# Attention windows in another order, long exponentials kept in PSUM, low weight parts on GpSimd

## The chip, the cores and the metric

The kernel runs on one core of a Trainium2 chip. A core has TensorE (matmuls into PSUM, with its own weight loads), VectorE, ScalarE, GpSimd, and SyncE, which issues DMAs. The metric is the device time of one execution in microseconds (us).

## What is computed

A block of a transformer on x of shape (2, 1024, 512): a layer norm, then multi-head latent attention with 32 heads and a gated feed-forward, whose sum is added to x. The change touches the attention alone:

```python
q = (_rms_norm(x @ wq_a.T, q_norm_w) @ wq_b.T).reshape(b, s, NH, QK_NOPE + QK_ROPE)   # 32 heads, 128 + 64
q_pe = _apply_rope(q_pe, cos, sin); k_pe = _apply_rope(k_pe, cos, sin)
scores = (jnp.einsum('bshd,bthd->bhst', q_nope, k_nope) + jnp.einsum('bshd,btd->bhst', q_pe, k_pe)) * scale
scores = jnp.where(causal, scores, finfo.min)
out = jnp.einsum('bhst,bthd->bshd', softmax(scores), v).reshape(b, s, NH * V_DIM)
return out @ wo.T
```

## The kernel before

Three parts follow one another: `dense` (norm, feed-forward, latents), `attention`, and `combine` (the output product). Attention uses the latent form: keys and values stay as a shared latent of 64 columns, and each head's query weights are multiplied with its key weights first.

The work of attention is cut into 32 windows of 8 steps (`WINS`, `WIN`, `STEPS` = 256). A window is a pair of heads with one of the two batches; window w is pair w % 16 with batch w // 16, so all pairs of the first batch come before the second. Steps u = 0 to 3 are the first head, 4 to 7 the second. A step handles two query tiles of 128 rows: a long one with 8 to 5 key tiles (1024, 896, 768, 640 columns) and a short one with 1 to 4 (128 to 512 columns), 9 key tiles in all.

For each step s the engines do, in programs written out by hand with semaphores:

- TensorE: `scores(s, LONG)` into one half of `score_long` (two banks of PSUM of four, by s % 2), `scores(s, SHORT)`, `transposes(s - 1)` of the short exponentials into `flip`, `values(s - 5)` (27 matmuls into `acc`), and at some steps a projection piece (`project`, five matmuls for 512 query columns into `proj`), the latent weights (`absorb`) and `output_weights`. The long scores of step s wait for the long exponential of step s - 2, which has then read that half.
- VectorE: `least` gives the row minimum of either tile (scores are negated, so it is the shift), `outputs` divides, `low_long(s - 1)` and `low_short(s - 1)` form the low half of the exponentials split in two fp16 numbers, and once a window `weights_low` does so for the query weights.
- ScalarE: `exp` of both tiles, `high_short(s - 1)` and `high_long(s)` copy the high halves, `take` brings a projection piece from `proj` to SBUF, `query_high` makes the high half of rotated queries, and `weights_latent` and `weights_high` build the weights two windows ahead.
- GpSimd: for each half k of a window's queries (k = 2p for places 0 and 1 of window p, 2p + 1 for places 2 and 3) four DMAs that swap rotation halves (`swap_halves`, which waits for the two takes), then `query_low(k - 1)`, and the rotation (multiplications by `sinT` and `cosT`, additions).
- SyncE: the transposing DMA of the long exponentials (`turn`), weight loads and stores.

A window's four pieces are its places 0 to 3. `PIECE` says at which step which is projected: `0: (1, 3)` means that in step 0 the piece of place 3 of the window after this one is done. `HIGH` gives the steps of `query_high` for the next window. The first scores of a window wait until all four low query parts are there (`pe.wait_ge(ql_ready, 4 * w)`).

## Time and profile before

| | us |
|---|---|
| runs of the kernel (3) | 1512.58, 1525.0, 1527.79; median 1525.0 |
| profiled execution | 1517.88, its span 1516.1 |
| busy in the span | PE 1320.1, weight loads 905.5, DVE 1102.5, ACT 955.1, POOL 776.8 |

The profile is of one execution. PE is TensorE, PEld its weight loads, DVE VectorE, ACT ScalarE, POOL GpSimd, SP SyncE; L859 is line 859 of the kernel. A matmul's row overlaps the next one's, since they are pipelined: the distance between two starts is what one costs. Times on VectorE and ScalarE also overlap by about 0.1 us from row to row.

### The profile page before, as it was taken

Reading aid. Unit: us, or ns where it says so; the run is one execution under the profiler, and the core shown is the slowest. Engines: PE = TensorE matmul, PEld = TensorE weight load, DVE = VectorE, ACT = ScalarE, POOL = GpSimd, SP = SyncE. Lnnn points to the kernel's source line nnn. Section 1 sums busy time; section 2 is a strip of 40 time slices with the busy share of each in tenths; the row PEclk is TensorE's granted clock in tenths of the full one; section 3 lists DMA queues with packets and bytes.
Section 4 is the critical chain, followed back from the end, with each engine's and each line's share of the span. In section 5 each row is a group of like instructions: output and inputs, shape, how many; then the busy total and the mean of one; then the engine's idle time right before and its main releaser. Section 6 shows DMA issues by size and latency. Waiting matters only on the chain. (4 is left out here: it accounts for less than half of the span.)

```text
span 1516.1 us, 32860 instructions
## 1 busy us (share of the span) xinstructions
PE 1320.1 (87%) x13058; PEld 905.5 (60%) x13058; DVE 1102.5 (73%) x1664; ACT 955.1 (63%) x1690; POOL 776.8 (51%) x759
## 2 busy tenths in 40 slices
PE   4899995988989998999988899999889898479997
PEld 4787773666666666666666666666666666334443
DVE  3755454788888888888888888888888889542321
ACT  3644433777777777777777777777777778641120
POOL 0222011777677767767766776776776674000110
PEclk8999997999999999999999999999999999889999
DMA  4011004788899888799898888979888897799995
GB/s 158 29 56 57 28 21 138 136 161 145 155 173 171 163 147 157 157 162 173 153 161 152 155 159 163 167 159 172 141 161 154 157 168 139 178 182 228 247 244 131
DMA packets 573641, 225.85 MB, mean 149 GB/s; under 512 B 509232, under 2 KB 552880, under 8 KB 572848
## 3 DMA queue, kind: packets, MB, share of 16 engines
q1 hardware_dynamic: 562992, 199.09, 68.3%
q0 software_dynamic: 10496, 24.66, 7.2%
q8 instruction: 104, 1.70, 0.5%
q14 instruction: 49, 0.40, 0.1%
HBM read 55.91 MB, written 25.17 MB: 53 GB/s over the span
## 5 line engine op out<-in xcount | busy, mean ns | idle before, releaser
L737 ACT ACTIVATE prob_long_sb<-score_long,shift_sb 128x1024 f32<-128x1024 f32 (+3 forms) x256 | 245.0, 957 | 250.0 <-DVE shift_sb L853 249.8
L859 DVE TENSOR_TENSOR prob_hl_sb<-prob_long_sb,prob_hl_sb 128x1024 f16<-128x1024 f32 (+3 forms) x256 | 358.0, 1398 | 0.0
L853 DVE TENSOR_REDUCE shift_sb<-score_long 128x1 f32<-128x1024 f32 (+3 forms) x256 | 259.4, 1013 | 68.1 <-PE score_long L649 67.6
L828 POOL TENSOR_TENSOR ql_sb<-qf_sb,qh_sb 128x512 f16<-128x512 f32 x124 | 144.8, 1169 | 233.9 <-ACT qh_sb L757 233.9
L745 ACT ACTIVATE prob_hl_sb<-prob_long_sb 128x1024 f16<-128x1024 f32 (+3 forms) x256 | 232.5, 908 | 0.0
L646 PE MATMUL score_long<-key_hi,qh_sb 128*128 128x512 f16 (+3 forms) x512 | 176.3, 344 | 10.0 <-DVE ql_sb L914 9.1
L659 PE MATMUL flip<-ident_sb,prob_short_sb 128*128 128x128 f32 x640 | 117.4, 281 | 73.9 <-DVE ptl_short_sb L865 73.7
L845 POOL TENSOR_TENSOR qf_sb<-qf_sb,rot_sb 64x512 f32<-64x512 f32 x124 | 174.1, 1404 | 9.5
L821 POOL DMA_DIRECT2D rot_sb<-qf_sb x248 | 124.8, 508 | 104.6 <-DVE ql_sb L914 61.3
L680 PE MATMUL acc<-ch,prob_t_sb 128*128 128x65 f16 x1664 | 177.5, 192 | 0.0
L678 PE MATMUL acc<-ch,prob_t_sb 128*128 128x65 f16 x1664 | 177.2, 194 | 0.3 <-DMA prob_t_sb<-prob_hl_sb 0.3
L679 PE MATMUL acc<-cl,prob_t_sb 128*128 128x64 f16 x1664 | 177.3, 191 | 0.0
L841 POOL TENSOR_TENSOR qf_sb<-qf_sb,cosT_sb 128x512 f32<-128x512 f32 x124 | 176.4, 1442 | 0.0
L647 PE MATMUL score_long<-key_lo,qh_sb 128*128 128x512 f16 (+3 forms) x512 | 174.6, 341 | 0.0
L648 PE MATMUL score_long<-key_hi,ql_sb 128*128 128x512 f16 (+3 forms) x512 | 171.1, 341 | 0.0
L680 PEld LDWEIGHTS acc<-ch,prob_t_sb 128*128 128x128 f16 x1664 | 153.1, 97 | 0.0
L679 PEld LDWEIGHTS acc<-cl,prob_t_sb 128*128 128x128 f16 x1664 | 152.7, 98 | 0.0
L678 PEld LDWEIGHTS acc<-ch,prob_t_sb 128*128 128x128 f16 x1664 | 152.2, 97 | 0.4 <-DMA prob_t_sb<-prob_hl_sb 0.4
L659 PEld LDWEIGHTS flip<-ident_sb,prob_short_sb 128*128 128x128 f32 x640 | 68.5, 140 | 115.9 <-issue 110.1
L865 DVE TENSOR_TENSOR ptl_short_sb<-flip,pth_short_sb 128x128 f16<-128x128 f32 (+3 forms) x256 | 123.9, 484 | 18.6 <-ACT pth_short_sb L752 9.7
L737 ACT ACTIVATE prob_short_sb<-score_short,shift_sb 128x128 f32<-128x128 f32 (+3 forms) x256 | 133.9, 523 | 0.0
L632 PE MATMUL proj<-lat_hi,wq_h_sb 128*128 128x512 f32 x246 | 107.2, 436 | 23.6 <-issue 22.9
(180 smaller groups left out, 3396.8 us busy)
## 6 DMA issues: line engine op xcount, KB each, us to landing
o<-o_sb SPq DMA_DIRECT2D x32, 512.0 KB, 4.5
o_nat_sb<-o SPq DMA_DIRECT2D x32, 512.0 KB, 6.8
rot_sb<-qf_sb POOLq DMA_DIRECT2D x248, 64.0 KB, 3.5
wqk_sb<-wqk SPq DMA_DIRECT2D x32, 320.0 KB, 4.4
wo_sb<-wo SPq DMA_DIRECT2D x16, 512.0 KB, 4.2
x_sb<-x SPq DMA_DIRECT2D x4, 1024.0 KB, 4.8
y<-y_sb SPq DMA_DIRECT2D x16, 256.0 KB, 2.0
wq_f_sb<-wqp SPq DMA_DIRECT2D x32, 128.0 KB, 4.5
```

What stands on the lines that cost most here:

```text
L646: nc.tensor.matmul(out, qh[:, row, q], key_hi[:, head, at], start=True, stop=False)
L647: nc.tensor.matmul(out, qh[:, row, q], key_lo[:, head, at], start=False, stop=False)
L659: mm = nc.tensor.transpose(flip[:, at], prob[SHORT][:, s % 2, at], ident[:])
L678: nc.tensor.matmul(acc[:, at:at + KVL + 1], hi, high, start=(j == 0), stop=False)
L679: nc.tensor.matmul(acc[:, at:at + KVL], hi, low, start=False, stop=False)
L680: mm = nc.tensor.matmul(acc[:, at:at + KVL + 1], lo, high, start=False, stop=(j == i))
L737: nc.scalar.activation(prob[kind][:, s % 2, 0:width(s, kind)], score_of(s, kind), ACT.Exp, bias=shift[:, s % (2 * WIN), kind:kind + 1], sc ...
L745: nc.scalar.activation(prob_hl[:, s % NHL, 0:n], prob[LONG][:, s % 2, 0:n], ACT.Copy).then_inc(hi_ready, 1)
L841: op = nc.gpsimd.tensor_tensor(qf[:, c, h, :], qf[:, c, h, :], cosT[:, h, at], ALU.mult)
L845: nc.gpsimd.tensor_tensor(qf[rows, c, h, :], qf[rows, c, h, :], rot[rows, c, :], ALU.add).then_inc(rot_add, 1)
L853: nc.vector.tensor_reduce(shift[:, s % (2 * WIN), kind:kind + 1], score_of(s, kind), AX.X, ALU.min).then_inc(shift_ready[kind], 1)
L859: nc.vector.tensor_tensor(prob_hl[:, s % NHL, n:2 * n], prob[LONG][:, s % 2, 0:n], prob_hl[:, s % NHL, 0:n], ALU.subtract).then_inc(lo_rea ...
```

## The change

- Window w is now pair w // 2 with batch w % 2. Both batches of a pair use the same query weights, so they are built (`absorb`, `weights_latent`, `weights_high`) in every second window (`new_pair`) and loaded half as often.
- The long exponential is written over its scores in PSUM. `prob_long` is gone, `high_long` and `low_long` read PSUM, and the long scores of a step wait for `lo_ready`, the long low part of the step two before.
- `weights_low` moves from VectorE to GpSimd, all but the first.
- `PIECE` puts places 0 and 1 at steps 4 and 6 instead of 3 and 4. Of these two pieces TensorE does three of five matmuls at the end of the step before (`BEGUN`).
- VectorE's order in a step becomes long minimum, long low part, short minimum, short low part, outputs. ScalarE's begins with `high_short(s - 1)`.

```diff
--- before.py
+++ after.py
@@ -483,7 +483,7 @@
...
-        prob = [sb("prob_short", [P, 2, 512], F32), sb("prob_long", [P, 2, S], F32)]
+        prob = sb("prob_short", [P, 2, 512], F32)
         prob_hl = sb("prob_hl", [P, NHL, 2 * S], F16)
...
@@ -521,8 +521,9 @@
...
-        PIECE = {0: (1, 3), 3: (2, 0), 4: (2, 1), 7: (2, 2)}
-        PIECE_FIRST = {0: (1, 2), 1: (1, 3), 4: (2, 0), 5: (2, 1), 7: (2, 2)}
+        PIECE = {0: (1, 3), 4: (2, 0), 6: (2, 1), 7: (2, 2)}
+        PIECE_FIRST = {0: (1, 2), 1: (1, 3), 4: (2, 0), 6: (2, 1), 7: (2, 2)}
+        BEGUN, TERMS = {4: 3, 6: 3}, 5
         HIGH = {1: (0,), 2: (1,), 5: (2,), 6: (3,)}
@@ -536,6 +537,11 @@
...
             return [4 * pair + n for n in (HIGH_FIRST if pair == 1 else HIGH).get(s % WIN, ())] if pair < WINS else []
+        def new_pair(w):
+            p = 1 if w == 0 else (w + 3) // 2 if w % 2 == 1 else PAIRS
+            return p if p < PAIRS else None
@@ -543,8 +549,8 @@
...
                 j = p % 2
-                sp.dma_start(raw[j][:].rearrange("p h c -> p (h c)"), io["wqk"][:, p % PAIRS, :]).then_inc(w_in[j], 16)
-                sp.dma_start(wf[j][:, :, KVL:KVL + 2 * ROPE], io["wqp"][:, p % PAIRS, :, :]).then_inc(w_in[j], 16)
+                sp.dma_start(raw[j][:].rearrange("p h c -> p (h c)"), io["wqk"][:, p, :]).then_inc(w_in[j], 16)
+                sp.dma_start(wf[j][:, :, KVL:KVL + 2 * ROPE], io["wqp"][:, p, :, :]).then_inc(w_in[j], 16)
@@ -570,7 +576,7 @@
...
                 sp.wait_ge(o_ready, BLK * (w + 1))
-                sp.dma_start(scr["o"][w % PAIRS, w // PAIRS], o[:, w % 2].rearrange("p t c -> p (t c)")).then_inc(o_out[w % 2], 16)
+                sp.dma_start(scr["o"][w // 2, w % 2], o[:, w % 2].rearrange("p t c -> p (t c)")).then_inc(o_out[w % 2], 16)
@@ -581,18 +587,18 @@
...
                 swap_halves(k)
-            for j in range(2):
-                sp.wait_ge(wl_ready, j + 1)
-                load_w(2 + j)
+            sp.wait_ge(wl_ready, 1)
+            load_w(2)
             for s in range(STEPS):
...
                     load_wo((w + 1) // 2)
-                if u == 3 and w + 4 < WINS:
-                    sp.wait_ge(wl_ready, w + 3)
-                    load_w(w + 4)
+                p = new_pair(w)
+                if u == 4 and p is not None and p + 2 < PAIRS:
+                    sp.wait_ge(wl_later, p)
+                    load_w(p + 2)
                 if u == LAG and w >= 1:
@@ -620,22 +626,23 @@
...
-            def project(n, out=proj[:]):
+            def project(n, out=proj[:], first=0, end=TERMS):
...
                 p, c, h = n // 4, n // 2 % 2, n % 2
-                b, j = p // PAIRS, p % 2
+                b, j = p % 2, p // 2 % 2
                 cols = slice(h * P, (h + 1) * P)
...
                 terms = ((wh, 0, lat_hi, 0), (wh, 0, lat_lo, 0), (wl, 0, lat_hi, 0), (wh, 1, lat_hi, 1), (wl, 1, lat_hi, 1))
-                for i, (w, t, q, kind) in enumerate(terms):
-                    mm = nc.tensor.matmul(out, w[j][:, t, cols], q[:, kind, at], start=(i == 0), stop=(i == 4))
-                mm.then_inc(proj_mm, 1)
+                for i, (w, t, q, kind) in list(enumerate(terms))[first:end]:
+                    mm = nc.tensor.matmul(out, w[j][:, t, cols], q[:, kind, at], start=(i == 0), stop=(i == TERMS - 1))
+                if end == TERMS:
+                    mm.then_inc(proj_mm, 1)
...
                 pair, head, i = s // WIN, s % WIN // BLK, tile(s, kind)
-                b = pair // PAIRS
+                b = pair % 2
                 q, row = slice(i * P, (i + 1) * P), 2 * (pair % 2) + head
@@ -656,11 +663,11 @@
...
                     at = slice(j * P, (j + 1) * P)
-                    mm = nc.tensor.transpose(flip[:, at], prob[SHORT][:, s % 2, at], ident[:])
+                    mm = nc.tensor.transpose(flip[:, at], prob[:, s % 2, at], ident[:])
                 mm.then_inc(flip_mm, 1)
...
             def values(s):
-                b = s // WIN // PAIRS
+                b = s // WIN % 2
                 for kind in (SHORT, LONG):
@@ -681,12 +688,9 @@
...
             absorb(0)
-            pe.wait_ge(lat_ready, 1)
-            absorb(1)
             pe.wait_ge(wl_ready, 1)
...
                 project(n, score_long[:, n, :])
-            pe.wait_ge(wl_ready, 2)
             project(4)
@@ -698,7 +702,7 @@
...
                     if s >= 2:
-                        pe.wait_ge(exp_ready[LONG], s - 1)
+                        pe.wait_ge(lo_ready, s - 1)
                     scores(s, LONG)
@@ -714,27 +718,34 @@
...
                     n = piece_at(s)
-                    if n is not None:
+                    if n is not None and u in BEGUN:
+                        project(n, first=BEGUN[u])
+                    elif n is not None:
+                        pe.wait_ge(proj_out, n)
+                        project(n)
+                    if u + 1 in BEGUN and piece_at(s + 1) is not None:
+                        n = piece_at(s + 1)
                         pe.wait_ge(proj_out, n)
                         if n % 4 == 0:
-                            pe.wait_ge(wl_ready, n // 4 + 1)
+                            pe.wait_ge(wl_later, n // 8)
                             pe.wait_ge(wo_ready, w + 1)
-                        project(n)
+                        project(n, end=BEGUN[u + 1])
                     if absorb_at(s):
...
                             pe.wait_ge(wo_ready, w)
-                        if w + 2 < WINS:
-                            absorb(w + 2)
+                        if new_pair(w) is not None:
+                            absorb(new_pair(w))
                         output_weights(w)
...
                 act.wait_ge(shift_ready[kind], s + 1)
-                if s >= 2:
-                    act.wait_ge(lo_ready if kind == LONG else flip_mm, s - 1)
-                nc.scalar.activation(prob[kind][:, s % 2, 0:width(s, kind)], score_of(s, kind), ACT.Exp,
+                if kind == SHORT and s >= 2:
+                    act.wait_ge(flip_mm, s - 1)
+                out = score_of(s, LONG) if kind == LONG else prob[:, s % 2, 0:width(s, SHORT)]
+                nc.scalar.activation(out, score_of(s, kind), ACT.Exp,
                                      bias=shift[:, s % (2 * WIN), kind:kind + 1], scale=-1.0).then_inc(exp_ready[kind], 1)
@@ -742,7 +753,7 @@
...
                 n = width(s, LONG)
-                nc.scalar.activation(prob_hl[:, s % NHL, 0:n], prob[LONG][:, s % 2, 0:n], ACT.Copy).then_inc(hi_ready, 1)
+                nc.scalar.activation(prob_hl[:, s % NHL, 0:n], score_of(s, LONG), ACT.Copy).then_inc(hi_ready, 1)
@@ -770,9 +781,8 @@
...
-            for p in range(2):
-                weights_latent(p)
-                weights_high(p)
+            weights_latent(0)
+            weights_high(0)
             for n in range(4):
@@ -783,10 +793,10 @@
...
                 w, u = s // WIN, s % WIN
+                if s >= 1:
+                    high_short(s - 1)
                 exp(s, LONG)
                 exp(s, SHORT)
-                if s >= 1:
-                    high_short(s - 1)
                 high_long(s)
@@ -799,12 +809,12 @@
...
                     act.wait_ge(vo_mm, w + 1)
-                    if w + 2 < WINS:
-                        weights_latent(w + 2)
+                    if new_pair(w) is not None:
+                        weights_latent(new_pair(w))
                     nc.scalar.activation(wo_out[:, w // 2, w % 2 * H // 2:(w % 2 + 1) * H // 2], of_out, ACT.Copy,
                                          scale=kvw2[:, 0:1]).then_inc(wo_ready, 1)
-                if high_weights_at(s) and w + 2 < WINS:
-                    weights_high(w + 2)
+                if high_weights_at(s) and new_pair(w) is not None:
+                    weights_high(new_pair(w))
             high_short(STEPS - 1)
@@ -828,6 +838,11 @@
...
+            def weights_low(p):
+                pool.wait_ge(wh_ready, p + 1)
+                nc.gpsimd.tensor_tensor(wl[p % 2][:], wf[p % 2][:], wh[p % 2][:].bitcast(F32),
+                                        ALU.subtract).then_inc(wl_later, 1)
             for k in range(2, 2 * WINS):
@@ -835,6 +850,8 @@
...
                     query_low(k - 1)
+                if c == 1 and new_pair(k // 2 - 1) is not None:
+                    weights_low(new_pair(k // 2 - 1))
                 pool.wait_ge(rot_in[c], 64 * (k // 2))
@@ -856,7 +873,7 @@
...
                 n = width(s, LONG)
-                nc.vector.tensor_tensor(prob_hl[:, s % NHL, n:2 * n], prob[LONG][:, s % 2, 0:n], prob_hl[:, s % NHL, 0:n],
+                nc.vector.tensor_tensor(prob_hl[:, s % NHL, n:2 * n], score_of(s, LONG), prob_hl[:, s % NHL, 0:n],
                                         ALU.subtract).then_inc(lo_ready, 1)
@@ -888,8 +905,7 @@
...
                 nc.vector.tensor_copy(to[:], of[:]).then_inc(cast_ready, 1)
-            for p in range(2):
-                weights_low(p)
+            weights_low(0)
@@ -918,15 +934,15 @@
...
                     least(s, LONG)
+                if 1 <= s <= STEPS:
+                    low_long(s - 1)
+                if s < STEPS:
                     least(s, SHORT)
+                if 1 <= s <= STEPS:
+                    low_short(s - 1)
                 t = s - LAG
...
                     outputs(t)
-                if 1 <= s <= STEPS:
-                    low_long(s - 1)
-                    low_short(s - 1)
-                if s < STEPS and high_weights_at(s) and w + 2 < WINS:
-                    weights_low(w + 2)
```

Where the rows move, engine by engine. First VectorE, the third step of a window (long tile of the step before 896 columns); L853 and L870 are `least`, L859 and L876 `low_long`. Before:

```order
L853 TENSOR_REDUCE shift_sb<-score_long 128x1 [waits score_long]
L853 TENSOR_REDUCE shift_sb<-score_short 128x1 [waits score_short]
L879 RECIPROCAL rtot_sb<-acc 128x4 [waits pv_mm]
L884 TENSOR_TENSOR o_sb<-acc,rtot_sb 128x2x2x64 [waits rtot_ready]
L859 TENSOR_TENSOR prob_hl_sb<-prob_long_sb,prob_hl_sb 128x896 [waits hi_ready]
L865 TENSOR_TENSOR ptl_short_sb<-flip,pth_short_sb 128x256 [waits pth_ready]
L870 TENSOR_TENSOR wq_l_sb<-wq_f_sb,wq_h_sb 128x512 [waits wh_ready]
```

Now:

```order
L870 TENSOR_REDUCE shift_sb<-score_long 128x1 [waits score_long]
L876 TENSOR_TENSOR prob_hl_sb<-score_long,prob_hl_sb 128x896 [waits hi_ready]
L870 TENSOR_REDUCE shift_sb<-score_short 128x1 [waits score_short]
L882 TENSOR_TENSOR ptl_short_sb<-flip,pth_short_sb 128x256 [waits pth_ready]
L896 RECIPROCAL rtot_sb<-acc 128x4 [waits pv_mm]
L901 TENSOR_TENSOR o_sb<-acc,rtot_sb 128x2x2x64 [waits rtot_ready,o_out1]
```

The long low part now stands behind the long minimum, ahead of the short one and of the outputs, takes its input from `score_long`, and the weights' row (before: L870) is gone.

Second ScalarE, from the take of place 0 or 1 in step 4 of a window to step 6 (L762 and L773 are `take`, L757 and L768 `query_high`, L752 and L763 `high_short`). Before, the first row is the take of place 1:

```order
L762 ACTIVATE qf_sb<-proj 128x512 [waits proj_mm,ql_ready]
L737 ACTIVATE prob_long_sb<-score_long,shift_sb 128x896 [waits lo_ready,shift_long]
L737 ACTIVATE prob_short_sb<-score_short,shift_sb 128x256 [waits flip_mm,shift_short]
L752 ACTIVATE pth_short_sb<-flip 128x128 [waits flip_mm,pv_mm]
L745 ACTIVATE prob_hl_sb<-prob_long_sb 128x896 [waits exp_long,turn_in1]
L757 ACTIVATE qh_sb<-qf_sb 128x512 [waits rot_add]
L737 ACTIVATE prob_long_sb<-score_long,shift_sb 128x768 [waits lo_ready,shift_long]
L737 ACTIVATE prob_short_sb<-score_short,shift_sb 128x384 [waits flip_mm,shift_short]
L752 ACTIVATE pth_short_sb<-flip 128x256 [waits flip_mm,pv_mm]
L745 ACTIVATE prob_hl_sb<-prob_long_sb 128x768 [waits exp_long,turn_in2]
L757 ACTIVATE qh_sb<-qf_sb 128x512 [waits rot_add]
```

Now, the first row is the take of place 0, and that of place 1 stands in step 6:

```order
L773 ACTIVATE qf_sb<-proj 128x512 [waits proj_mm,ql_ready]
L763 ACTIVATE pth_short_sb<-flip 128x128 [waits flip_mm,pv_mm]
L748 ACTIVATE score_long<-score_long,shift_sb 128x896 [waits shift_long]
L748 ACTIVATE prob_short_sb<-score_short,shift_sb 128x256 [waits flip_mm,shift_short]
L756 ACTIVATE prob_hl_sb<-score_long 128x896 [waits exp_long,turn_in1]
L768 ACTIVATE qh_sb<-qf_sb 128x512 [waits rot_add]
L763 ACTIVATE pth_short_sb<-flip 128x256 [waits flip_mm,pv_mm]
L748 ACTIVATE score_long<-score_long,shift_sb 128x768 [waits shift_long]
L748 ACTIVATE prob_short_sb<-score_short,shift_sb 128x384 [waits flip_mm,shift_short]
L756 ACTIVATE prob_hl_sb<-score_long 128x768 [waits exp_long,turn_in2]
L773 ACTIVATE qf_sb<-proj 128x512 [waits proj_mm,ql_ready]
L768 ACTIVATE qh_sb<-qf_sb 128x512 [waits rot_add]
```

The take of place 1 has moved behind the long high copy of step 6, ahead of the last `query_high`; the short high copy leads each step. GpSimd's own order around these is unchanged: the four DMAs that wait for this take, then the two `query_low` of the window to come, and now in every second window `weights_low` behind the pair of `query_low` in its middle.

Third TensorE, where the pieces of a new window begin, at the end of step 3. Before:

```order
L632 MATMUL proj<-lat_hi,wq_h_sb 128x512 [waits wo_ready,wl_ready,proj_out]
L632 MATMUL proj<-lat_lo,wq_h_sb 128x512
L632 MATMUL proj<-lat_hi,wq_l_sb 128x512
L632 MATMUL proj<-lat_hi,wq_h_sb 128x512
L632 MATMUL proj<-lat_hi,wq_l_sb 128x512
L646 MATMUL score_long<-key_hi,qh_sb 128x512 [waits exp_long]
```

Now:

```order
L638 MATMUL proj<-lat_hi,wq_h_sb 128x512 [waits wo_ready,wl_later,proj_out]
L638 MATMUL proj<-lat_lo,wq_h_sb 128x512
L638 MATMUL proj<-lat_hi,wq_l_sb 128x512
L653 MATMUL score_long<-key_hi,qh_sb 128x512 [waits lo_ready]
L654 MATMUL score_long<-key_lo,qh_sb 128x512
```

Three of the five matmuls stand ahead of the scores of step 4, with the wait for the low weights (`wl_later`, set by GpSimd), and the scores wait for `lo_ready` in place of `exp_long`. The first scores of a window wait for `ql_ready` too, as before.

## Rows read from the trace of the kernel before

**Rows 1.** Busy time of each engine in one stretch of attention, 100 us long.

```profile
core 0: us, PE busy (x) PEld busy (x) DVE busy (x) ACT busy (x) POOL busy (x), PEclk, DMA share, GB/s
500.00:600.00 100.00, 90.28 (x1077) 62.81 (x1075) 87.14 (x126) 76.10 (x133) 70.29 (x66) 1.00 0.88 163
```

**Rows 2.** Timeline of TensorE, one window: start us, us, instruction, [idle before it].

```profile
586.80 0.39 PE L646 MATMUL score_long<-key_hi,qh_sb 128*128 128x512 f16 x1
...
588.10 0.22 PE L649 MATMUL score_long<-mask_b_sb,ident_b_sb 128*128 128x128 bf16 x1
...
589.64 0.47 PE L632 MATMUL proj<-lat_hi,wq_h_sb 128*128 128x512 f32 x1
...
590.90 0.39 PE L646 MATMUL score_long<-key_hi,qh_sb 128*128 128x512 f16 x1
...
593.88 1.08 PE L611 MATMUL proj<-wqk_sb 128*128 128x64 f32 x8
594.89 0.65 PE L619 MATMUL proj<-wo_sb,wv_sb 128*64 128x256 f32 x4
595.47 0.39 PE L646 MATMUL score_long<-key_hi,qh_sb 128*128 128x512 f16 x1
...
598.10 0.38 PE L646 MATMUL score_long<-key_hi,qh_sb 128*128 128x512 f16 x1
...
619.71 0.39 PE L646 MATMUL score_long<-key_hi,qh_sb 128*128 128x512 f16 x1
```

**Rows 3.** Waits of TensorE, 200 to 1400 us: total us, times, longest.

```profile
PE flip L659 <- DVE ptl_short_sb L865: 73.7, 157, 1.8
```

**Rows 4.** Costliest groups, whole run, then by form, 400 to 1300 us.

```profile
L859 DVE TENSOR_TENSOR prob_hl_sb<-prob_long_sb,prob_hl_sb 128x1024 f16<-128x1024 f32 (+3 forms) x256 | 358.0, 1398 | 0.0
...
L859 DVE TENSOR_TENSOR prob_hl_sb<-prob_long_sb,prob_hl_sb 128x640 f16<-128x640 f32 x55 | 97.9, 1780 | 0.0
...
L865 DVE TENSOR_TENSOR ptl_short_sb<-flip,pth_short_sb 128x512 f16<-128x512 f32 x55 | 37.3, 678 | 0.3 <-ACT pth_short_sb L752 0.2
```

**Rows 5.** Timeline of VectorE in the last window, GpSimd idle.

```profile
1290.06 1.22 DVE L853 TENSOR_REDUCE shift_sb<-score_long 128x1 f32<-128x1024 f32 x1
...
1292.34 0.82 DVE L859 TENSOR_TENSOR prob_hl_sb<-prob_long_sb,prob_hl_sb 128x640 f16<-128x640 f32 x1
...
1295.14 1.21 DVE L859 TENSOR_TENSOR prob_hl_sb<-prob_long_sb,prob_hl_sb 128x1024 f16<-128x1024 f32 x1
...
1298.83 1.08 DVE L859 TENSOR_TENSOR prob_hl_sb<-prob_long_sb,prob_hl_sb 128x896 f16<-128x896 f32 x1
...
1301.49 0.94 DVE L859 TENSOR_TENSOR prob_hl_sb<-prob_long_sb,prob_hl_sb 128x768 f16<-128x768 f32 x1
```

**Rows 6.** Timeline of ScalarE and GpSimd, steps 4 to 6 of the window.

```profile
609.90 0.60 ACT L762 ACTIVATE qf_sb<-proj 128x512 f32<-128x512 f32 x1
...
610.80 2.01 POOL L821 DMA_DIRECT2D rot_sb<-qf_sb  x4 [1.39 <-ACT qf_sb L762]
...
616.75 0.66 ACT L757 ACTIVATE qh_sb<-qf_sb 128x512 f16<-128x512 f32 x1
...
617.48 1.16 POOL L828 TENSOR_TENSOR ql_sb<-qf_sb,qh_sb 128x512 f16<-128x512 f32 x1 [1.62 <-ACT qh_sb L757]
```

**Rows 7.** Timeline of VectorE and ScalarE in step 6.

```profile
614.37 0.55 DVE L853 TENSOR_REDUCE shift_sb<-score_short 128x1 f32<-128x384 f32 x1
...
615.28 0.60 ACT L737 ACTIVATE prob_short_sb<-score_short,shift_sb 128x384 f32<-128x384 f32 x1
...
616.01 0.87 ACT L745 ACTIVATE prob_hl_sb<-prob_long_sb 128x768 f16<-128x768 f32 x1
```

**Rows 8.** Timeline of TensorE and ScalarE in the first window.

```profile
271.18 0.38 PE L646 MATMUL score_long<-key_hi,qh_sb 128*128 128x512 f16 x1
...
274.50 0.63 ACT L771 ACTIVATE wq_h_sb<-wq_f_sb 128x512 fp32r<-128x512 f32 x1
...
290.88 0.39 PE L646 MATMUL score_long<-key_hi,qh_sb 128*128 128x512 f16 x1 [0.74 <-POOL ql_sb L828]
```

2 lines of the change are left out of this document (1 added, 1 removed).

## Prediction

> **What bounds the kernel now.** I read the table of stretches first, then TensorE's own rows step by step, then the waits. Attention is 256 steps; eight steps are one window (a head pair with one batch), and it is nearly the whole span between about 256 and 1310 us. In a stretch of it TensorE is busy 90%, VectorE 87%, ScalarE 76%, GpSimd 71%, with TensorE's clock granted in full [rows 1]. No engine is full, so I looked for what repeats. The window from 586.80 to 619.71 takes 32.91 us [rows 2], and the windows around it take the same within 0.1 us. I number its steps 0 to 7. Step 0 takes 4.10 us with one projection piece, step 2 takes 2.63 us, and both run without a wait. A piece costs 1.26 us (589.64 to 590.90), the latent weights 1.01 us, the output weights 0.58 us [rows 2]. Every step has the same number of score and value columns and differs only in 1 to 4 transposes: from 4.10 - 1.26 = 2.84 us with four and 2.63 us with two, a step without extras is 2.84, 2.52, 2.63, 2.74 us. Two of each, four pieces (5.04), 1.01 and 0.58 give 28.1 us. So 4.8 us of each window are waits. The largest named one is for VectorE's short low parts [rows 3]. VectorE is late because its subtraction of the long low parts is slow while GpSimd works: 1398 ns in the mean, 1780 ns for 640 columns [rows 4], against 0.82 us for the same shape after GpSimd's last rotation [rows 5].
>
> **VectorE.** The subtraction now reads the long exponentials in PSUM. Its nearest row is the same operation for the short tile, PSUM in, 678 ns for 512 columns [rows 4], no slower a column than the undisturbed long rows once the fixed part is taken off. Below them I see no reason for a gain; above, the 1.40 us of now would be the other end, were it PSUM and not GpSimd's company that counts. I take the undisturbed durations of [rows 5]: 1.21, 1.08, 0.94 and 0.82 us for 1024 down to 640 columns, where the mean over the attention is 1.40 [rows 4]. That frees 0.39 us a step, 3.1 us a window, and the low weights leave VectorE too, which is then no bound.
>
> **TensorE.** Sharing weights between the two batches drops the latent weights in every second window: 28.1 becomes 27.6 us on average. The pieces are the same work in other places: step 3 gets three of five matmuls (0.76 us), step 4 two (0.50), 5 and 6 likewise, steps 7 and 0 a whole one.
>
> **The new hold on the scores.** Scores of step s+1 now wait for the long low part of step s-1, and not for an exponential. VectorE does this part right behind the minimum of step s, which waits for the scores of step s. So one step can't be shorter than long scores, minimum, subtraction. Long scores take 1.52 us at 1024 columns (586.80 to the mask row's end at 588.32) and 0.16 less a tile [rows 2]; the minimum takes 1.22 us for 1024 [rows 5] and like the subtraction for the others. With 0.11 us for handoffs and overlap (an estimate), steps 0 to 3 need 3.67, 3.76, 3.34 and 2.90 us, and 4 to 7 the same. Taking the larger of this and TensorE's own work: 4.11, 3.76, 3.34, 3.50, 3.67, 3.76, 3.34, 4.00, in all 29.5 us, and 0.35 more in every second window, where step 1 holds the latent weights. ScalarE's work is 25 us of it (76% of 32.9, [rows 1]) and loses half of its weight copies, so it isn't the bound. If nothing else stood in the way, 29 windows would save 3.2 us each, some 93 us.
>
> **What stands in the way.** One move undoes this. GpSimd issues the four swap DMAs of a pair only when its places 0 and 1 are taken, and does the low query parts of the next window behind them. Before, place 1 was taken in step 4: ScalarE ended at 610.50, the DMAs began at 610.80 and took 2.01 us, and the two low parts (1.16 us each) then waited only for ScalarE's high parts and ended at 618.64, 1.07 us before the next window's scores at 619.71 [rows 6]. Now place 1 is taken in step 6. Behind this take lie 0.30 us to GpSimd, 2.01 us for the DMAs and 2 x 1.16 us, and scores of the next window wait for all four low parts. Step 6 begins 22.1 us into the window by the sum above (22.5 in every second). In it come scores (1.24 with the handoff), minimum 0.95, subtraction 1.08, short minimum 0.55, short exponential 0.60, high copy 0.85, take 0.60, less 0.37 for rows that begin before the former's end: 5.5 us [rows 2, 5, 7]. To this the 4.63 us of GpSimd and about 0.15 to TensorE. The next window begins at 22.1 + 5.5 + 4.8 = 32.4 us, or 32.8 us. TensorE would stand for some 3 us at each window's start, and of 3.2 us only about 0.35 us remain: 29 windows of 32.91 us, 954.4 us, become 14 x 32.4 + 15 x 32.76 = 945, so some 10 us are won.
>
> **The ends.** In the first window the three terms of step 3 wait for the low weights, now on GpSimd behind its two low query parts and not on VectorE. The high weights of [rows 8] end at 275.1 and come half a microsecond later in the new order; GpSimd ends at about 278.1. And this wait now stands ahead of the scores of step 4, which were at 271.18. I get 279.0 for them, 286.4 for step 6 and, with the same tail of 10.3 us, 296.7 for the second window, where it was 290.88 [rows 8]: 5.8 us lost. The window before the last has no later take and wins 0.5 us; the last, where nothing disturbed VectorE before, loses about 1.5 us to the hold. Sum: -10 + 5.8 - 0.5 + 1.5 = -3 us. Against the profiled execution (1517.9 us, its span 1516.1) that is 1515 us; that execution lies inside the runs (median 1525.0), from which it would be 1522. I predict **1518 us**. Anything within 1% of 1525 is no change that a measurement of this kernel can tell.
>
> **Bounds of what no row shows.** No instruction in the trace writes PSUM from ScalarE. Nearest are its copies and exponentials that read PSUM: the exponential on 384 columns takes 0.60 us [rows 7]. A write in place could cost nothing more, or, if reading and writing the same banks take turns, the time again. Below nothing I exclude more than some 0.05 us each, the scale of fixed parts in these rows. I take nothing. The Trainium skill, "ScalarEngine: Activation LUTs", section on what happens when an exp runs, says PSUM is the lower-latency destination for ScalarE; no row shows it, and it would leave the sum where it is, since the long exponential of step 6 is ready 0.6 us before it is needed. GpSimd's low weights are bounded by its own two-input rows, 1.16 us [rows 6], and hidden in the middle of a window. Each of the dozen handoffs on the ring may be off by 0.03 us: 0.4 us a window, 12 us in all.
>
> **Rivals.** (1) *The ring through GpSimd has slack that I don't see*, say because the low parts aren't needed or the take is earlier. Then the windows run at 29.7 us: 1518 - 93 = 1425 us. For it speaks that VectorE's relief is certain; against it, the order of GpSimd's instructions, and that this very wait shows once already: the scores at 290.88, ahead of which both low parts came late, stood 0.74 us for them [rows 8]. Chance 0.08. (2) *Slower: the exponential in place costs double.* Its four shapes average some 0.95 us, so ScalarE gets 7.6 us more per window, 25 becomes near 32, and the take of step 6, the end of ScalarE's chain, comes 1 to 2 us late. It decides from the point where the long exponential costs over 0.6 us more. 29 x 1.5 = 44: 1562 us. Chance 0.08. (3) *The hold is longer than I make it*: the subtraction has to wait for ScalarE's high copy in steps 2, 3 and 6, where I find only 0.2 to 0.5 us to spare. For it speaks that the copy of short tiles now stands ahead of both exponentials; against it, that ScalarE is idle a quarter of the time [rows 1]. +0.9 us a window, 1544 us. Chance 0.10. (4) *TensorE has room*: if its rows overstate it, the steps 0 and 3, where I let its own work decide, shrink to the hold (3.67, 2.90), 1.0 us a window before the ring: 1489 us. Against it stand step 0 and step 2, whose rows lie end to end. Chance 0.06. The Trainium skill, "Perfetto Trace Analysis", on identifying the most-contended engine, would have TensorE judged by weight loads, and [rows 1] have them at 63% beside 90% for matmuls: by that rule (4) it is. (5) *Ring right, quicker round*: my walk is too long by 0.4 us a window or more: 1495 to 1508 us, chance 0.13. My forecast, 1508 to 1540, has the remaining 0.55.
>
> **How the numbers follow.** Faster by over 1% (below 1510): cases 1, 4, 5 and a sliver of mine, 0.28. Slower by over 1% (above 1540): case 2 and most of 3, 0.16. Within: 0.56. The range reaches over (3) and (4) and leaves (1) and (2) out: 1484 to 1548.
>
> **What would show it.** In the profile after: each window near 32.5 us; TensorE idle some 3 us before the long scores of every eighth step, released by GpSimd's low query part; the swap DMAs right behind the take of step 6, and the low parts right behind them; the long subtraction at 0.82 to 1.21 us; VectorE near 75% busy; GpSimd's multiplications shorter, since nothing disturbs them; the first window near 40 us. The prediction is wrong if windows are near 29.5 us without that idle time, or if the long exponentials take well over 1.1 us at 1024 columns.

## The result and the profile after

The changed kernel takes 1563.2 us, median of 4 runs (1558.66 to 1569.87), against 1524.9 us of the kernel before (4 runs, 1512.58 to 1527.79): a ratio of 1.027, 95% interval 1.0212 to 1.0328. It is slower, and outside the range that was given. Its profiled execution took 1561.21 us, span 1559.4. Here and below a median is that of all runs of a kernel, and a ratio leaves out the few that were in a slower state of the chip.

The table of stretches of the changed kernel: the one that answers to [rows 1], and 3.2 us of two windows:

```profile
core 0: us, PE busy (x) PEld busy (x) DVE busy (x) ACT busy (x) POOL busy (x), PEclk, DMA share, GB/s
500.00:600.00 100.00, 89.79 (x1039) 63.11 (x1038) 70.14 (x117) 73.19 (x126) 64.36 (x68) 0.96 0.85 157
...
598.40:601.60 3.20, 3.20 (x38) 3.12 (x36) 2.98 (x6) 1.68 (x3) 2.52 (x3) 0.51 0.47 91
632.10:635.30 3.20, 3.20 (x44) 2.46 (x42) 3.12 (x6) 2.42 (x4) 0.42 (x1) 1.00 0.90 75
```

VectorE fell from 87% to 70% busy, and TensorE stays at 90%. The same share hides that it did less: 1039 matmuls where there were 1077. And the granted clock is no longer full. Both short stretches begin 1.5 us after a window's first scores and show TensorE fully busy, but the granted clock is 0.51 in the first (1.2 GHz) and 1.00 in the second (2.4 GHz). Full busy time says nothing of the speed.

TensorE's timeline at the same two places (the answer to [rows 2]), where each first row opens a window and each second one opens its step 1:

```profile
596.88 0.39 PE L653 MATMUL score_long<-key_hi,qh_sb 128*128 128x512 f16 x1 [2.48 <-POOL ql_sb L838]
...
602.57 0.39 PE L653 MATMUL score_long<-key_hi,qh_sb 128*128 128x512 f16 x1
...
630.59 0.39 PE L653 MATMUL score_long<-key_hi,qh_sb 128*128 128x512 f16 x1 [2.48 <-POOL ql_sb L838]
...
634.67 0.39 PE L653 MATMUL score_long<-key_hi,qh_sb 128*128 128x512 f16 x1
```

Both windows open after the same 2.48 us without work, released by GpSimd's low query part, as the prediction has it. But step 0, with the same work, takes 5.69 us behind the first and 4.08 behind the second. In 26 of the 29 windows from the second to the thirtieth it is the longer one. The record of the clock shows a dip, of some 3.4 us (6.8 in one), in each of these 26. The kernel before shows none between 290 and 1314 us; its waits of about the same sum (4.8 us a window) lie in pieces of 1.9 us or less.

The round through GpSimd itself (called the ring below: take, four swap DMAs, two low query parts, next scores), in the window from 630.59 to 663.12 (timeline of ScalarE, GpSimd and TensorE, beside [rows 6]):

```profile
657.89 0.60 ACT L773 ACTIVATE qf_sb<-proj 128x512 f32<-128x512 f32 x1
...
658.77 2.00 POOL L831 DMA_DIRECT2D rot_sb<-qf_sb  x4 [3.46 <-ACT qf_sb L773]
...
660.79 2.27 POOL L838 TENSOR_TENSOR ql_sb<-qf_sb,qh_sb 128x512 f16<-128x512 f32 x2
...
663.12 0.61 PE L653 MATMUL score_long<-key_hi,qh_sb 128*128 128x512 f16 x1 [2.49 <-POOL ql_sb L838]
```

The take of place 1 ends at 658.49, and 4.63 us later the next window's scores begin. GpSimd's two low parts follow the four DMAs without a gap, so the wait is this queue and nothing else. In one window, from 764.83, GpSimd starts its four DMAs late without a cause that the profile names (797.66, 3.3 us behind the take's end at 794.37); it takes 3.0 us more than its like. The trace of before has the same 3.3 us once, at 778.45.

The long subtraction and the exponential (groups of the whole run, then by form, 400 to 1200 us, beside [rows 4] and [rows 5]):

```profile
L876 DVE TENSOR_TENSOR prob_hl_sb<-score_long,prob_hl_sb 128x1024 f16<-128x1024 f32 (+3 forms) x256 | 259.6, 1014 | 2.0 <-ACT prob_hl_sb L756 2.0
L748 ACT ACTIVATE score_long<-score_long,shift_sb 128x1024 f32<-128x1024 f32 (+3 forms) x256 | 238.8, 933 | 18.0 <-DVE shift_sb L870 17.7
...
L748 ACT ACTIVATE score_long<-score_long,shift_sb 128x1024 f32<-128x1024 f32 x47 | 51.1, 1087 | 0.0
...
L876 DVE TENSOR_TENSOR prob_hl_sb<-score_long,prob_hl_sb 128x640 f16<-128x640 f32 x47 | 38.3, 814 | 0.0
```

The subtraction takes 1014 ns in the mean where it was 1398, and 814 for 640 columns where it was 1780. The exponential in place costs nothing more (933 ns in the mean, 957 before).

The first window on TensorE, beside [rows 8]:

```profile
250.69 0.59 PE L653 MATMUL score_long<-key_hi,qh_sb 128*128 128x512 f16 x1 [9.14 <-DVE ql_sb L930]
...
272.45 0.77 PE L638 MATMUL proj<-lat_hi,wq_h_sb 128*128 128x512 f32 x1 [6.64 <-POOL wq_l_sb L843]
273.87 0.65 PE L653 MATMUL score_long<-key_hi,qh_sb 128*128 128x512 f16 x1
...
292.59 0.39 PE L653 MATMUL score_long<-key_hi,qh_sb 128*128 128x512 f16 x1 [2.49 <-POOL ql_sb L838]
```

**The account**, by starts of windows in the two profiled executions, changed against before. The first scores come at 250.69, not 256.33: -5.6 us. The first window takes 41.90, not 34.55: +7.4. The 29 windows after it take 983.05, not 955.94: +27.1. With step 0 at 4.1 us in all of them they would take some 941 (983.1 less 26 x 1.6, an estimate), fewer than before. The last two come to -0.3. The output part behind attention takes 216.6 us, not 201.8: +14.8. In all 43.3, the difference of the spans.

### The profile page after: what moved, and what is told of

Same layout as the page of the kernel before. It is cut to its first block and busy times, and to the rows that moved or that the text cites. A ratio compares the mean times of both kernels' runs of the same rounds, so it can differ in the third digit from the quotient of the medians.

```text
span 1559.4 us, 32254 instructions
## 1 busy us (share of the span) xinstructions
PE 1334.1 (86%) x12930; PEld 907.7 (58%) x12930; DVE 956.4 (61%) x1633; ACT 950.7 (61%) x1658; POOL 721.4 (46%) x774
## 5 line engine op out<-in xcount | busy, mean ns | idle before, releaser
L870 DVE TENSOR_REDUCE shift_sb<-score_long 128x1 f32<-128x1024 f32 (+3 forms) x256 | 261.7, 1022 | 311.6 <-PE score_long L656 307.9
L876 DVE TENSOR_TENSOR prob_hl_sb<-score_long,prob_hl_sb 128x1024 f16<-128x1024 f32 (+3 forms) x256 | 259.6, 1014 | 2.0 <-ACT prob_hl_sb L756 2.0
L748 ACT ACTIVATE score_long<-score_long,shift_sb 128x1024 f32<-128x1024 f32 (+3 forms) x256 | 238.8, 933 | 18.0 <-DVE shift_sb L870 17.7
L763 ACT ACTIVATE pth_short_sb<-flip 128x128 f16<-128x128 f32 (+3 forms) x256 | 112.5, 440 | 190.0 <-PE flip L666 187.2
L756 ACT ACTIVATE prob_hl_sb<-score_long 128x1024 f16<-128x1024 f32 (+3 forms) x256 | 221.5, 865 | 0.3
L653 PEld LDWEIGHTS score_long<-key_hi,qh_sb 128*128 128x128 f16 x512 | 50.3, 98 | 238.4 <-POOL ql_sb L838 91.2
L654 PE MATMUL score_long<-key_lo,qh_sb 128*128 128x512 f16 (+3 forms) x512 | 182.1, 356 | 0.0
L655 PE MATMUL score_long<-key_hi,ql_sb 128*128 128x512 f16 (+3 forms) x512 | 180.2, 358 | 0.0
L862 POOL TENSOR_TENSOR qf_sb<-qf_sb,rot_sb 64x512 f32<-64x512 f32 x124 | 157.0, 1266 | 9.5
L858 POOL TENSOR_TENSOR qf_sb<-qf_sb,cosT_sb 128x512 f32<-128x512 f32 x124 | 155.7, 1278 | 0.0
L1030 PE MATMUL sum<-woh_sb,oT_sb 128*128 128x512 f16 x256 | 100.2, 391 | 26.9 <-DMA oT_sb<-o_hl_sb 26.1
```

Source lines behind the costliest of these rows:

```text
L653: nc.tensor.matmul(out, qh[:, row, q], key_hi[:, head, at], start=True, stop=False)
L654: nc.tensor.matmul(out, qh[:, row, q], key_lo[:, head, at], start=False, stop=False)
L655: nc.tensor.matmul(out, ql[:, row, q], key_hi[:, head, at], start=False, stop=not last)
L748: nc.scalar.activation(out, score_of(s, kind), ACT.Exp, bias=shift[:, s % (2 * WIN), kind:kind + 1], scale=-1.0).then_inc(exp_ready[kind], 1)
L756: nc.scalar.activation(prob_hl[:, s % NHL, 0:n], score_of(s, LONG), ACT.Copy).then_inc(hi_ready, 1)
L858: op = nc.gpsimd.tensor_tensor(qf[:, c, h, :], qf[:, c, h, :], cosT[:, h, at], ALU.mult)
```

## The experiments

The kernel before ran beside each group of four: 1523.6, 1523.4 and 1521.8 us. Where a run is called "with pieces back" it is this one:

**Pieces back at their old steps.** Everything of the change stays but the fourth point of its list, the one on `PIECE` (the first window's pieces and the waits go with it).

```diff
-        PIECE = {0: (1, 3), 4: (2, 0), 6: (2, 1), 7: (2, 2)}
...
-        BEGUN, TERMS = {4: 3, 6: 3}, 5
+        PIECE = {0: (1, 3), 3: (2, 0), 4: (2, 1), 7: (2, 2)}
...
+        BEGUN, TERMS = {}, 5
...
                         pe.wait_ge(proj_out, n)
+                        if n % 4 == 0:
+                            pe.wait_ge(wl_later, n // 8)
+                            pe.wait_ge(wo_ready, w + 1)
                         project(n)
```

> The changed kernel with the projection pieces back at steps 0, 3, 4 and 7, whole, and nothing else undone. Theory (ring and clock: the take of place 1 in step 6 delays the swap DMAs and the low query parts behind it, TensorE stands 2.84 us at each window's start and then runs some 3.4 us at half clock, 1.6 us more): no wait for the low query parts, clock 1.00 throughout attention, steps of 4.1, 3.7 or 4.1, 3.3, 4.0, 4.1, 3.7, 3.3, 4.0 us, windows of 30.3 us where the changed kernel has 33.7 and 34.15. 29 windows x 3.65 = 106 us and 6 us of the first window: about 1450 us. Rival (the hold on the score banks is what costs): windows stay near 33 us or above, 1530 us or more.

Measured: 1459.6 us (0.957 of before, 0.952 to 0.961). Its windows take 30.47 and 30.90 us in turn, TensorE doesn't wait for a low query part at a window's start (0.3 us once, at the second), and its clock is 1.00 from 400 to 1200 us. So two pieces placed later cost 103.6 us, which is more than the whole loss. Between the spans it is 109.2, and the 29 windows hold 93.5 of it.

**The same move by itself in the kernel before.**

```diff
-        PIECE = {0: (1, 3), 3: (2, 0), 4: (2, 1), 7: (2, 2)}
...
+        PIECE = {0: (1, 3), 4: (2, 0), 6: (2, 1), 7: (2, 2)}
...
+        BEGUN, TERMS = {4: 3, 6: 3}, 5
...
```

> The kernel before with this one part of the change alone: places 0 and 1 in steps 4 and 6, three of five matmuls a step early. Ring theory: the same wait for the low query parts at each window's start, the same half clock behind it, windows of 35 to 36 us where they were 32.9: 1590 to 1615 us. Rival (the ring needs the other parts of the change): within 1% of 1525 us.

Measured: 1617.6 us (1.061, 1.055 to 1.066). From its trace, a window's first step:

```profile
653.91 0.39 PE L648 MATMUL score_long<-key_hi,qh_sb 128*128 128x512 f16 x1 [2.12 <-POOL ql_sb L836]
...
659.59 0.39 PE L648 MATMUL score_long<-key_hi,qh_sb 128*128 128x512 f16 x1
```

Much the same wait (2.12 us for 2.48) and 5.68 us behind it. Step 0 is the slow one in 17 of 29 windows; the other 12 took 4.10 there. The move costs 94 us here and 104 above: most of its cost doesn't depend on the rest of the change.

**The clock alone: work in the idle time.** In step 7 the piece is computed three times; only the third counts. The ring stays.

```diff
-            def project(n, out=proj[:], first=0, end=TERMS):
+            def project(n, out=proj[:], first=0, end=TERMS, signal=True):
...
-                if end == TERMS:
+                if end == TERMS and signal:
                     mm.then_inc(proj_mm, 1)
...
                         pe.wait_ge(proj_out, n)
+                        for _ in range(2 if u == 7 else 0):
+                            project(n, signal=False)
                         project(n)
```

> The changed kernel with its wait left in, and TensorE does the piece of step 7 three times over (ten more matmuls of 0.23 us, the same values into the same bank, only the last signalled), so that it isn't idle for more than about 0.4 us of the 2.84. If the clock is what makes step 0 cost 5.7 in place of 4.1 us: the granted clock stays at 1.00, step 0 is back at 4.1 us, windows near 32.3 us, 1563 - 26 x 1.6 = 1521 us, though TensorE has 2.5 us more work in each window. Rival (step 0 is slow for another reason, such as the DMAs of that time, or the wait grows by the extra work): no gain or a loss, 1563 us or more.

Measured: 1525.7 us (1.0008 of before, 0.998 to 1.0037), 37.6 us less than the changed kernel though TensorE does more. Its stretch and the first two steps of a window:

```profile
500.00:600.00 100.00, 96.26 (x1123) 67.60 (x1122) 73.60 (x124) 77.25 (x131) 68.63 (x71) 1.00 0.86 162
```

```profile
616.01 0.39 PE L653 MATMUL score_long<-key_hi,qh_sb 128*128 128x512 f16 x1 [0.19 <-POOL ql_sb L840]
...
620.10 0.39 PE L653 MATMUL score_long<-key_hi,qh_sb 128*128 128x512 f16 x1
```

Step 7 still lasts 6.88 us (6.84 in the changed kernel), so the ring sets the same time. But step 0 is back at 4.09, and the 29 windows take 943.8 us where the changed kernel's take 983.1. The 39.3 us between are the clock's price, 1.5 us for each of the 26 slow steps. The prediction had 945 us for these windows. It described this kernel, not the changed one. That it is met within 1.2 us is in part luck: the regular windows take 32.15 and 32.58 us, 0.2 less than predicted, and one stretch with GpSimd's late start (35.56 and 33.78 us, with a half-clock step) gives 5 us back.

**Low parts ahead of the DMAs.** On GpSimd, the last two low query parts of the next window go first, and the swap DMAs of the window after it follow.

```diff
+                if k > 2 and c == 0:
+                    query_low(k - 1)
                 swap_halves(k)
-                if k > 2:
+                if k > 2 and c == 1:
                     query_low(k - 1)
```

> The changed kernel with its pieces where they are, but GpSimd does the two low query parts of a window ahead of the four swap DMAs of the next (for the halves with places 0 and 1). Ring and clock theory: the low parts then wait only for the last high part of step 6, TensorE's wait at a window's start falls from 2.8 us to 0.1 or nothing, the clock stays, windows of 29.6 us: 1563 - 29 x 4.35 = 1437 us. Rival (TensorE waits there because the take, or GpSimd as a whole, is late): some 1 to 2 us of the wait stay and windows are near 32 us, 1510 us.

Measured: 1535.4 us (1.0065, 1.003 to 1.010), a miss of nearly 100 us. The wait at the window's start went (step 7 4.20 us, step 0 4.10), but step 3 now takes 4.5 to 11.2 in 27 of 29 windows, and the granted clock falls at 13 of these waits too. GpSimd and then ScalarE in its trace:

```profile
583.57 1.17 POOL L838 TENSOR_TENSOR ql_sb<-qf_sb,qh_sb 128x512 f16<-128x512 f32 x1 [2.71 <-ACT qh_sb L768]
584.67 2.01 POOL L831 DMA_DIRECT2D rot_sb<-qf_sb  x4
594.84 1.27 POOL L858 TENSOR_TENSOR rot_sb<-rot_sb,sinT_sb 128x512 f32<-128x512 f32 x1 [8.16 <-DMA rot_sb<-qf_sb]
...
598.63 2.59 POOL L864 TENSOR_TENSOR qf_sb<-qf_sb,rot_sb 64x512 f32<-64x512 f32 x2
```

```profile
599.92 0.63 ACT L768 ACTIVATE qh_sb<-qf_sb 128x512 f16<-128x512 f32 x1 [5.59 <-POOL qf_sb L864]
```

The DMAs leave at a window's end, land up to 8 us later, the rotation follows, and ScalarE stands at `query_high` in step 1 with all exponentials behind it. I had looked at one side of the queue only.

**The same, with `query_high` of places 0 and 1 a step later.**

```diff
-        HIGH = {1: (0,), 2: (1,), 5: (2,), 6: (3,)}
+        HIGH = {2: (0,), 3: (1,), 5: (2,), 6: (3,)}
```

> The changed kernel with the two low query parts ahead of the swap DMAs (which alone gave 1535.4 us and an irregular wait of 4.5 to 11 us in step 3), and ScalarE's query_high of places 0 and 1 one step later (steps 2 and 3, not 1 and 2). If that wait is ScalarE standing at query_high because the swap DMAs leave only in step 7 and land up to 8 us later, it shrinks by one step, 3.3 us: windows mostly at 29.9 to 31 us and the kernel at 1445 to 1470 us. Rival: the irregular wait has another source (the DMA queues, TensorE's clock); then it stays and the time is again near 1535 us.

Measured: 1455.3 us (0.954, 0.948 to 0.960). Step 3 is regular again (3.7 us), and every second window takes 29.91 us. The others take 29.46 at best and up to 32.9: their step 7 takes 4.2 to 7.6, where ScalarE stands at the `query_high` of step 5 behind DMAs that land late. So the wait in step 3 was ScalarE's place in that queue. 29.46 and 29.91 are the window that the prediction gave without anything in the way (29.5, and 29.85 every second).

**Pieces split, from the walk.** Pieces back, but three of five matmuls of those in steps 3 and 7 are done a step earlier, where the hold left TensorE idle.

```diff
-        BEGUN, TERMS = {}, 5
+        BEGUN, TERMS = {3: 3, 7: 3}, 5
```

> The changed kernel with the pieces back at their old steps 0, 3, 4 and 7, but three of the five matmuls of the pieces of steps 3 and 7 done at the end of steps 2 and 6. In the run with whole pieces at these steps, steps 2 and 6 took 3.25 us, which is the hold on the score banks (TensorE's own work there is 2.63), and steps 3 and 7 took 4.20, which is TensorE's own work. If the walk of the prediction holds (each step the larger of hold and own work), steps 2 and 6 become 3.4 and steps 3 and 7 some 3.5, so a window 30.7 - 1.1 = 29.6 us and the kernel 1459.6 - 29 x 1.1 = 1428 us. Rival: the round through GpSimd binds at once when windows shrink; then the windows stay above 30.3 and the kernel at 1448 or more, with TensorE waiting for the low query part again and its clock falling behind that.

Measured: 1423.6 us (0.934, 0.927 to 0.940), windows 29.10 and 29.53.

**And place 1 over steps 4 and 5.**

```diff
-        PIECE = {0: (1, 3), 3: (2, 0), 4: (2, 1), 7: (2, 2)}
-        BEGUN, TERMS = {3: 3, 7: 3}, 5
+        PIECE = {0: (1, 3), 3: (2, 0), 5: (2, 1), 7: (2, 2)}
+        BEGUN, TERMS = {3: 3, 5: 3, 7: 3}, 5
```

> As the run before (pieces split over 2 and 3, 6 and 7), and place 1 spread over steps 4 and 5, taken in step 5 and no longer in step 4. The take moves one step, not two as in the changed kernel. The ring of the prediction from a take in step 5 (it starts at about 18.1 us of the window): take's end about 5.9 us later, 0.30, 2.01, 2 x 1.16, 0.15: 28.8 us, below the window of 29.1 that the hold and TensorE's own work give. So no wait at the window's start, 0.4 us a window less than the run before: 1428 - 12 = 1416 us. Rival: the swap DMAs, which now leave 4 us later, land too late for the rotation behind them (in the trace with low parts first they took up to 8 us), query_high then holds ScalarE, and the kernel comes out above 1440 us.

Measured: 1414.6 us (0.927, 0.921 to 0.932), the fastest of all. A window of 29.06 us on TensorE, without idle time ahead of either row:

```profile
577.90 0.39 PE L653 MATMUL score_long<-key_hi,qh_sb 128*128 128x512 f16 x1
...
606.96 0.39 PE L653 MATMUL score_long<-key_hi,qh_sb 128*128 128x512 f16 x1
```

One step later fits into the ring, two steps don't. Its matmuls are 98% busy from 500 to 600 us. The idea of spreading the pieces was sound; the place of one take was not.

**What the other parts bring.** Four more runs, which lead from the kernel before to the one with pieces back. First the orders of VectorE and ScalarE alone:

```diff
                     least(s, LONG)
+                if 1 <= s <= STEPS:
+                    low_long(s - 1)
+                if s < STEPS:
                     least(s, SHORT)
...
+                if s >= 1:
+                    high_short(s - 1)
                 exp(s, LONG)
                 exp(s, SHORT)
-                if s >= 1:
-                    high_short(s - 1)
```

> The kernel before with only the new orders: VectorE long minimum, long low part, short minimum, short low part, outputs; ScalarE with the short high copy first. Windows, weights, pieces and the long exponentials in SBUF stay as they were. The run with pieces back and long exponentials in SBUF (1463.8 us) has these orders, shared weights and low weights on GpSimd over before, 60 us in all. Theory 1, the orders bring most of it, since the short low parts for which TensorE's transposes waited 73.7 us come earlier: 1475 to 1490 us. Theory 2, VectorE's load is what counts (87% busy, low weights in every window), and an order adds nothing to it: 1510 to 1530 us.

Measured: 1524.6 us (1.0017, 0.9996 to 1.0038). No gain, theory 2. Added to it, the exponential in place:

```diff
-                        pe.wait_ge(exp_ready[LONG], s - 1)
+                        pe.wait_ge(lo_ready, s - 1)
...
+                out = score_of(s, LONG) if kind == LONG else prob[SHORT][:, s % 2, 0:width(s, SHORT)]
...
```

> The run before this one (the new orders alone) with the long exponential written over its scores in PSUM, and the long scores waiting for the low part. VectorE then has the subtraction at 1010 ns and not 1400, 3 us a window, while its low weights are still there in every window. Theory of the prediction: VectorE's time was the bound, the hold sets 29.5 to 31 us a window, with whole pieces in steps 3 and 4 near 31: 1524 - 29 x 1.9 = about 1470 us. Rival: in the kernel with shared weights and pieces back the same step changed nothing (1463.8 to 1459.6); if that is general, this run equals the one with the orders alone.

Measured: 1504.9 us (0.989, 0.986 to 0.992): 20 us, not the 54 expected and not nothing. Its steps are those of the longer windows of the run with pieces back but for step 3, 5.68 us for 4.20. There TensorE stands ahead of the next pair's first piece until VectorE has made the low weights, which it does in every window here:

```profile
561.73 1.23 DVE L871 TENSOR_TENSOR wq_l_sb<-wq_f_sb,wq_h_sb 128x512 fp32r<-128x512 f32 x1 [1.50 <-ACT wq_h_sb L772]
...
563.07 0.47 PE L632 MATMUL proj<-lat_hi,wq_h_sb 128*128 128x512 f32 x1 [1.02 <-issue]
```

Then, with pieces back, the long exponentials in SBUF:

```diff
-                        pe.wait_ge(lo_ready, s - 1)
+                        pe.wait_ge(exp_ready[LONG], s - 1)
...
-                out = score_of(s, LONG) if kind == LONG else prob[:, s % 2, 0:width(s, SHORT)]
+                out = prob_long[:, s % 2, 0:width(s, LONG)] if kind == LONG else prob[:, s % 2, 0:width(s, SHORT)]
...
```

> The run with the pieces back at their old steps (1459.6 us), with the long exponentials in SBUF again: the subtraction reads two SBUF inputs, and the long scores wait for an exponential and not for the low part. If the exponentials in PSUM pay by VectorE's relief, the subtraction is back at some 1400 ns in the mean (1780 for 640 columns) and the windows go from 30.7 to about 31.9 us (the old 32.9, less 0.9 of low weights that stay on GpSimd, 0.1 of shared weights): 1459.6 + 35 = 1495 us. Rival: the hold on the score banks costs as much as the relief gives; then steps 5 and 6 fall from 3.69 and 3.25 to near TensorE's own 2.7 and the kernel is at 1455 us or below.

Measured: 1463.8 us (0.960, 0.953 to 0.966), against 1459.6, and the two kernels' runs overlap: neither theory. By form, 400 to 1200 us, this kernel's subtraction:

```profile
L880 DVE TENSOR_TENSOR prob_hl_sb<-prob_long_sb,prob_hl_sb 128x640 f16<-128x640 f32 x53 | 72.0, 1359 | 0.0
L880 DVE TENSOR_TENSOR prob_hl_sb<-prob_long_sb,prob_hl_sb 128x1024 f16<-128x1024 f32 x52 | 67.6, 1299 | 0.0
...
L880 DVE TENSOR_TENSOR prob_hl_sb<-prob_long_sb,prob_hl_sb 128x768 f16<-128x768 f32 x52 | 49.5, 952 | 0.0
```

The relief is real but smaller than in the kernel before, 0.2 us in the mean (1207 ns against 1014) and not 0.39, and the hold takes it back: in place, steps 2 and 5 take 3.25 and 3.68 us where they take 2.6 (in every second window) and 2.5 in SBUF, while step 3 falls from 5.5 and 4.8 to 4.2. Next that kernel with the low weights back on VectorE:

```diff
-                if c == 1 and new_pair(k // 2 - 1) is not None:
-                    weights_low(new_pair(k // 2 - 1))
...
-            def weights_low(p):
+            def weights_low(p, done=wl_ready):
...
+                if s < STEPS and high_weights_at(s) and new_pair(w) is not None:
+                    weights_low(new_pair(w), wl_later)
```

> The run with pieces back and the long exponentials in SBUF (1463.8 us), with the low parts of the query weights on VectorE again, in every second window, at the end of its step 2. This undoes the move to GpSimd alone. VectorE was 84% busy there; 0.9 to 1.3 us in 16 windows, half of it on the path: 1464 + 8 to 1464 + 20, so 1472 to 1484 us. Rival: GpSimd, which is on the ring, pays as much for it as VectorE does: no difference, 1460 to 1467 us.

Measured: 1477.5 us (0.972, 0.967 to 0.978); the move to GpSimd is worth 14 us. What is left between this run and the one with the orders alone, 1524.6 - 1477.5 = 47 us, is shared weights. From its trace, the two waits of TensorE in a window that builds weights:

```profile
618.46 0.39 PE L654 MATMUL score_short<-key_hi,qh_sb 128*128 128x512 f16 x1 [1.38 <-ACT prob_short_sb L752]
...
624.77 0.23 PE L654 MATMUL score_short<-key_hi,qh_sb 128*128 128x128 f16 x1 [1.67 <-ACT prob_short_sb L752]
```

Windows take 29.78 us without weights and 33.0 with them. The latent weights' own 1.01 us on TensorE is a third of that. The rest lies in steps 3 and 4 (5.53 and 5.94 us, not 4.78 and 4.09), at the late short exponentials of these rows, behind the work that the weights bring to ScalarE and VectorE. Which part of that work makes them late was not tested. Last, the fastest kernel with its long exponentials in SBUF (the edit of the run above):

> The fastest kernel so far (pieces split over 2 and 3, 4 and 5, 6 and 7; 1414.6 us) with its long exponentials in SBUF again and the old wait. With pieces whole the two placements were equal (1463.8 and 1459.6), since steps 3 and 7 took 4.2 us of TensorE's own work or more in either. Theory: VectorE in that form is 84% busy at 30.4 us a window, so a window of 28.8 us would want 88% and its steps wait for short exponentials and low parts; windows stay at 30 us or more: 1450 us or above. Rival: without the hold steps 1, 2, 5 and 6 (3.4 to 3.7 us, TensorE's own work below) get shorter, and the kernel is at 1415 us or less.

Measured: 1478.7 us (0.970, 0.963 to 0.977; runs from 1469.6 to 1493.1), 55 us or more above the fastest. The exponential in place gave 4 us with whole pieces, inside the spread of the runs, and gives 55 to 64 with split ones: it pays where the steps are short. That VectorE's load is the reason is the expectation's argument, and no edit here isolates it.

## Why the prediction was wrong

**The step that failed** is the last of "What stands in the way": "TensorE would stand for some 3 us at each window's start, and of 3.2 us only about 0.35 us remain". It charges the idle time and nothing for what follows it. The clock fell behind this idle in 26 of 29 windows, and step 0 then took 5.7 us for 4.1. That no rival had it is why the range ended at 1548. The run with filled idle time shows it: 943.8 us for 29 windows, with 945 predicted and 983.1 in the changed kernel. Between the spans the change cost 43.3 us where the sum had won 3. Of these 46 us, 37 are in the 29 windows and 15 in the output part; the start of attention and its last two windows give 5 back.

No row of the regular windows of before priced this, since they kept the full clock. But half-clock stretches stood in its output part, behind waits, and one in its first window, right behind a wait of 1.66 us. I took none of them as a warning:

```profile
275.98 0.47 PE L632 MATMUL proj<-lat_hi,wq_h_sb 128*128 128x512 f32 x1 [1.66 <-issue]
```

```profile
276.50:279.90 3.40, 3.40 (x10) 1.56 (x9) 3.01 (x4) 2.85 (x5) 3.40 (x3) 0.50 0.00 0
```

**The ring was right**, term by term. In the window from 630.59, step 6 starts 22.43 us in (22.5), the take ends 5.47 later (5.5), and the next scores 4.63 after that (4.78). The three windows that kept the clock take 32.53 to 32.55 us (32.8 predicted); rival 5 wanted 0.4 us less, not 0.25.

**The hold was right, the sum in part by luck.** In the best windows of the run with `query_high` a step later, steps 0 to 7 take 4.10, 3.68, 3.25, 3.73, 3.58, 3.68, 3.25, 4.20, in all 29.47 us; predicted 4.11, 3.76, 3.34, 3.50, 3.67, 3.76, 3.34, 4.00, in all 29.5. The steps that the hold sets came 0.1 us shorter each, and steps 3 and 7, where TensorE's own work decides, 0.2 longer. Rival 3 falls, and so does rival 4: steps 0 and 3 never went below TensorE's own work as I summed it, though weight loads are 63% busy as before. By the Trainium skill, "Perfetto Trace Analysis", "Identifying the Most-Contended Engine", weight loads and the matmul throughput should have been the measure, and not the busy share of matmuls. The loads disagree with the steps here: in the fastest run they are 69% busy where matmuls are 98%.

**VectorE was right in size** (1014 ns, with the undisturbed durations taken), and the price of the exponential in place too: 1087 ns at 1024 columns against 1119 in SBUF in the run with pieces back and long exponentials in SBUF. Rival 2 falls; its time, 1562 us, is met by accident and by another cause. On PSUM as the lower-latency destination of ScalarE (the Trainium skill, "ScalarE: Activation LUTs", "Step-by-step: what each stage is for") the rows agree, by 32 ns.

**Rival 1** describes windows without the wait: the kernel with pieces back, or with low parts first and `query_high` later. Its 1425 us takes off 93 us although the forecast had already counted 10 of them; it should have been some 1434. At 1455 to 1460 us both runs are above either, since whole pieces make windows of 30.7 us in the one and late DMAs 30.2 in the other.

**The ends.** First window: I had +5.8 us and the second window at 296.7. It started at 292.59, +1.7. What I missed is that all of it starts 5.6 us earlier: one pair's weights are built ahead of it, no longer two. The last two windows: +1.0 predicted, -0.3 measured. The output part behind them, whose code is untouched, I set at nothing; it took 14.8 us more. This part is open. It spans 201.8 us (before) to 222.2 (filled idle time) in fourteen traces whose code there is the same, with other DMA landings and half-clock stretches in each. The four with pieces in steps 4 and 6 and this change have 216.6 to 222.2, the ten others 201.8 to 214.8. The profiled execution of before was also 7 us faster than its median. The run with filled idle time is no faster there, so the dips in attention are not the cause. I can't say which share the change has.

## To carry to other kernels

Price an idle gap on TensorE with what its clock does behind it, even if no gap so long is in the profile. Two microseconds and a half in one piece cost a microsecond and a half more in 26 of 29 windows here, while as much idle time in small pieces cost only itself. And before moving a step past a queue, walk the round that leads through it for each place it could go to: one step later cost nothing, two cost about 100 us.
